# The edge stage of a graph network kernel: gathered rows turned by VectorE and spread by 16 small DMAs instead of being transposed on TensorE

## What is computed

```python
h = maximum(layernorm(x), 0)                       # x: 50000 x 128
gs, gp, gd = rbf @ w_rs, (rbf @ w_rp) * pij, (rbf @ w_rd) * dij    # per edge: 12500 edges, rbf 32, pij 3, dij 5
xx = resmlp0(h)                                    # every node
xs, xp, xd = resmlp1(h)[idx_j], resmlp2(h)[idx_j], resmlp3(h)[idx_j]   # per edge
s = xx + segment_sum(gs * xs, idx_i)
p = segment_sum(gp * xp, idx_i);  d = segment_sum(gd * xd, idx_i)
pa, pb = split(p @ w_pp);  da, db = split(d @ w_pd)
y = s + (pa * pb).sum(-2) + (da * db).sum(-2)
out = x + resmlp4(y)
# resmlp(x) = silu(x + silu(silu(x) @ w1 + b1) @ w2 + b2) @ wout
```

## Time and profile before

| | |
|---|---|
| time, median of 3 runs | 1169.51 us (1167.19 to 1170.66) |
| profiled execution, first to last instruction | 1167.6 us |
| PE, DVE, ACT, POOL busy | 95%, 54%, 65%, 40% of the span |
| node stage | about 0 to 362 us |
| start of the edge stage, PE nearly still | 362 to 379 us |
| edge stage, 25 groups | 379 to 832 us |
| border totals, late blocks and final stage | 832 to 1167.6 us |

### The profile page before, as it was taken

One profiled execution on the slowest core, in us unless ns is written; L12 is line 12 of the kernel. 1 busy time (PEld: TensorE's weight loads), 2 busy tenths in 40 slices (PEclk: granted clock), 3 DMA queues, 4 the chain that ended last, 5 costly groups with the idle time before them and its releaser, 6 DMA issues.

```text
span 1167.6 us, 22917 instructions
## 1 busy us (share of the span) xinstructions
PE 1106.1 (95%) x6787; PEld 751.3 (64%) x6787; DVE 635.5 (54%) x2304; ACT 757.1 (65%) x1423; POOL 463.0 (40%) x426
## 2 busy tenths in 40 slices
PE   3799999899995899999999999999889999999998
PEld 2466766677773466676666666767556666666665
DVE  9999885878762456556565565565512222222222
ACT  2488999789995565655655656555356666666654
POOL 3077773077775346556555565563500000000000
PEclk9999999999998899999999999999999999999999
DMA  8389779477755033333333333334357878888774
GB/s 261 106 264 346 255 254 314 167 232 252 259 180 141 25 66 60 64 59 47 55 49 54 59 50 54 58 44 87 60 176 253 263 254 263 260 249 264 266 241 149
DMA packets 163582, 191.51 MB, mean 164 GB/s; under 512 B 58050, under 2 KB 82538, under 8 KB 163359
## 3 DMA queue, kind: packets, MB, share of 16 engines
q1 hardware_dynamic: 125166, 145.35, 40.6%
q0 software_dynamic: 24208, 19.29, 10.1%
q10 hardware_dynamic: 14112, 25.70, 5.8%
HBM read 94.06 MB, written 96.20 MB: 163 GB/s over the span
## 4 chain that ended last, share of the span: by engine, by line
PE 86%; DVE 9%; DMA 2%; issue 2%; ACT 1%; POOL 0%; SPq 0%; POOLq 0%; ACTq 0%; DVEq 0%
PE bank L1035 8%; PE quad L1023 7%; PE bank L1593 6%; PE bank L858 6%; PE quad L841 6%; PE quad L1027 5%; PE bank L1603 5%; PE bank L1667 4%; PE quad L848 4%; PE bank L1635 4%; PE bank L1668 4%; PE quad L1012 3%; DVE stat L521 2%; PE quad L826 2%; DVE onehot L633 2%; PE quad L1677 2%
## 5 line engine op out<-in xcount | busy, mean ns | idle before, releaser
L1247 POOL DMA_INDIRECT node_sums<-rowout,row_i x98 | 154.9, 1581 | 188.1 <-ACT rowout L1509 165.6
L952 DVE TENSOR_TENSOR rowout<-bank,xin 128x512 f32<-128x512 f32 x98 | 67.8, 692 | 248.7 <-PE bank L1035 248.7
L1035 PEld LDWEIGHTS bank<-wo_sb,s 128*128 128x128 f32 x784 | 102.8, 192 | 47.7 <-issue 47.7
L1280 DVE SCALAR_TENSOR_TENSOR h<-bank,b_sb,hT 128x512 f32<-128x512 f32 (+1 forms) x75 | 55.5, 740 | 138.9 <-PE bank L1603 138.9
L465 POOL DMA_INDIRECT edges_by_src<-pay,rank_i x98 | 99.8, 1019 | 70.9 <-DVE rank_i L662 42.0
L465 POOL DMA_INDIRECT edges_by_low<-pay,rank_i x98 | 98.3, 1003 | 62.1 <-DVE rank_i L662 32.2
L858 PEld LDWEIGHTS bank<-wo_sb,s 128*128 128x128 f32 x720 | 94.7, 192 | 42.9 <-issue 42.9
L751 ACT ACTIVATE xn<-xin,nbias,rnorm 128x128 f32<-128x128 f32 x216 | 103.6, 491 | 14.8 <-DVE nbias L572 14.7
L72 POOL DMA_INDIRECT yin<-node_h,er x98 | 94.7, 967 | 38.1 <-issue 29.2
L1035 PE MATMUL bank<-wo_sb,s 128*128 128x128 f32 x784 | 103.5, 275 | 0.9 <-DVE rowout L952 0.9
L1023 PE MATMUL quad<-s,w_sb 128*128 128x512 f32 x196 | 101.7, 601 | 0.1
(11 more groups left out here) (208 smaller groups left out, 2313.2 us busy)
## 6 DMA issues: line engine op xcount, KB each, us to landing
xin<-in_x_dram SPq DMA_DIRECT2D x196, 256.0 KB, 3.2
node_h<-xn SPq DMA_DIRECT2D x98, 256.0 KB, 2.8
yin<-node_sums SPq DMA_DIRECT2D x98, 256.0 KB, 3.6
out_dram<-rowout ACTq DMA_DIRECT2D x98, 256.0 KB, 3.5
node_sums<-rowout SPq DMA_DIRECT2D x90, 256.0 KB
border_sums_by_tile<-border_sums SPq DMA_DIRECT2D x24, 256.0 KB, 2.0
node_sums<-zeros SPq DMA_DIRECT2D x8, 256.0 KB
edges_by_low<-pay,rank_i POOLq DMA_INDIRECT x98
```

The lines of the kernel that those rows point to most:

```text
L1035: last = nc.tensor.matmul(BANK_O[:, j * P:(j + 1) * P], s3[:, s, j * P:(j + 1) * P], wo_sb[:, m, :], start=True, stop=True)
L1247: nc.gpsimd.indirect_dma_start(out=ysum, out_offset=bass.IndirectOffsetOnAxis(ap=row_i[:, t % 2, j:j + 1], axis=0), in_=urow[:, t % 2, j, ...
```

## The change

Only the edge stage changes in what it does.

- PE no longer transposes gathered rows (except those of group 0), nor the edge features, nor runs the four `pick_src` matmuls.
- DVE turns the gathered rows of group k+1 in 32x32 squares into a new tile `xq` (`squares_T`), at the start of iteration k, ahead of `residual(k,0)`. SP then moves the 4x4 grid of turned squares with 16 SBUF-to-SBUF DMAs (`spread`), each 32 partitions x 128 words, into `hT`. The columns of `hT` now run through the tiles in turn (edge 0 of tiles 0 to 3, edge 1, ...), so what reads a tile's columns as weights (`halves`, `outp(k,2)`), and the two `gate` copies, do so with a step of 4 words.
- `rb` is replaced by `rq`, loaded by one DMA per tile so that DVE's 32x32 transposes make `eR` and `eA` from it directly (`features_T`).
- The sources come as a row: at the start of the stage one DMA copies the 12,544 source words of the table into a DRAM row, word by word, and per group one DMA brings 512 of them to all partitions (`src_in_every_row`).
- The final stage takes over semaphores of the node stage instead of new ones.

```diff
 def load_group(...):
-    eng.dma_start(er[:, s, 0:n, 0:C], rows[:, :, 0:C]).then_inc(indices, 16)
-    eng.dma_start(rb[:, s, 0:n, :], rows[:, :, C:W]).then_inc(done, 16)
+    eng.dma_start(er[:, s, 0:n, :], rows[:, :, 0:C]).then_inc(indices, 16)
+    for t in range(n):
+        tile = by_src[start + t * P:start + (t + 1) * P, :].rearrange("(q r) w -> r q w", r=Q)
+        eng.dma_start(rq[t * Q:(t + 1) * Q, s, :, :], tile).then_inc(done, 16)
...
     def sync(sp):
+        def spread(k):
+            if 1 <= k < G:
+                h, e = k % 2, tiles(k) * Q
+                sp.wait_ge(xq_done, k)
+                if k >= 2:
+                    sp.wait_ge(s1_done, k - 1)
+                    sp.wait_ge(h2_done, 3 * (k - 1))
+                for q in range(P // Q):
+                    for c in range(P // Q):
+                        sp.dma_start(hT[c * Q:(c + 1) * Q, h, q * e:(q + 1) * e],
+                                     xq[q * Q:(q + 1) * Q, h, c * e:(c + 1) * e]).then_inc(hT_in[h], 16)
...
+        def load_src_row(k):
+            if k < G:
+                s, e = k % 2, tiles(k) * P
+                if k >= 2:
+                    sp.wait_ge(same_done, k - 1)
+                sp.dma_start(srow[:, s, 0:e], src_row[0:1, k * BLOCK:k * BLOCK + e].to_broadcast([P, e])).then_inc(srow_in[s], 16)
...
+            sp.dma_start(src_row[0, :].rearrange("(t p) -> t p", p=P), by_src[0:T * P, 0:1].rearrange("(t p) w -> t (p w)", p=P),
+                         allow_slow_non_contiguous=True).then_inc(keys_in, 16)
...
         for k in range(G + 1):
+            spread(k + 1)
             store(k - 2)
             load(k + 2)
+            if k == 0:
+                sp.wait_ge(keys_in, 64)
+                load_src_row(0)
+            load_src_row(k + 1)
...
     def vector(dve):
-        def take_h(k):
+        def squares_T(k):
+            if 1 <= k < G:
+                s, n = k % U, tiles(k)
+                dve.wait_ge(x_in[s], 16 * (TB * (k // U) + n))
+                if k >= 3:
+                    dve.wait_ge(hT_in[k % 2], hT_there(k - 2))
+                nc.vector.transpose(xq[:, k % 2, 0:n * P].rearrange("p (c r t) -> p t c r", t=n, r=Q),
+                                    xg[:, s, 0:n, :].rearrange("p t (c r) -> p t c r", r=Q)).then_inc(xq_done, 1)
...
         for k in range(G + 1):
             t = k - 1
+            squares_T(k + 1)
             if k == 0:
                 key_masks()
             residual(k, 0)
...
-            take_h(k + 1)
+            features_T(k + 1)
...
     def tensor(pe):
-            rows_T(k + 1)
-            edges_T(k + 1)
             outp(k, 2)
...
-                nc.tensor.matmul(BANK_AB[:, 0:2 * F], mT[:, t % 2, 0, cols], wpp_sb[:, :], ...)
+                nc.tensor.matmul(BANK_AB[:, 0:2 * F], by_tile(mT[:, t % 2, 0, 0:n * P], n)[:, j], wpp_sb[:, :], ...)
```

More of the change, by code:

```diff
@@ L190, in rows_there @@
         def rows_there(k):
-            return 48 * (k // U + 1) - (0 if k % U else 16)
+            each = 16 * (TB + 2)
+            short = 16 * (TB - (T - k * TB)) if k == G - 1 and T - k * TB < TB else 0
+            return each * (k // U + 1) - (0 if k % U else 16) - short
         gathered = [sem(f"gathered{i}") for i in range(U)]
@@ L1162, in edge_phase @@
                          "sum_done", "u_in_psum", "u_done", "row_steps", "rows_done"))
+    quads_T, xq_done = sem("edge_features_T"), sem("gathered_quads_T")
+    hT_in = [sem(f"hT_in{i}") for i in range(2)]
+    srow_in = [sem(f"src_row_in{i}") for i in range(2)]
     key_ps, key_done, item_rows, item_ps, item_c, item_steps, item_done = (
@@ L1207, in load_items @@
                 sp.dma_start(items_s[lo:hi, side, :], ssum[lo:hi, side, :]).then_inc(done, 16)
+        with nc.allow_non_contiguous_dma(reason="one word of each row"):
+            sp.dma_start(src_row[0, :].rearrange("(t p) -> t p", p=P), by_src[0:T * P, 0:1].rearrange("(t p) w -> t (p w)", p=P),
+                         allow_slow_non_contiguous=True).then_inc(keys_in, 16)
         with nc.allow_non_contiguous_dma(reason="first and last key of each tile"):
@@ L1476, in gates @@
                 n = tiles(k)
-                for m in range(3):
-                    last = nc.scalar.copy(gate[:, m, 0:n * P].rearrange("p (t e) -> p t e", t=n), quad[:, 0:n, m * P:(m + 1) * P])
-                last.then_inc(gate_done, 1)
+                for m in range(2):
+                    nc.scalar.copy(by_tile(gate[:, m, 0:n * P], n), quad[:, 0:n, m * P:(m + 1) * P])
+                nc.scalar.copy(gate[:, 2, 0:n * P].rearrange("p (t f) -> p t f", t=n), quad[:, 0:n, 2 * P:3 * P]).then_inc(gate_done, 1)
         def halves(t, j):
@@ L1637, in outp @@
                     for j in range(tiles(k)):
-                        last = nc.tensor.matmul(BANK_O[:, j * P:(j + 1) * P], s3[:, m, j * P:(j + 1) * P], wo_sb[:, MLP[m], :], start=True, stop=True)
+                        last = nc.tensor.matmul(BANK_O[:, j * P:(j + 1) * P], by_tile(s3[:, m, 0:tiles(k) * P], tiles(k))[:, j], wo_sb[:, MLP[m], :],
+                                                start=True, stop=True)
                 last.then_inc(o_done, 1)
@@ L1651, in seg @@
                     rows = slice(j * Q, (j + 1) * Q)
-                    nc.tensor.matmul(quad[:, j, 0:2 * P], eA[rows, q, :], ePD[rows, q, :, :].rearrange("p a e -> p (a e)"),
-                                     start=True, stop=True, skip_group_check=True)
-                for j in range(tiles(t)):
-                    rows = slice(j * Q, (j + 1) * Q)
-                    last = nc.tensor.matmul(quad[:, j, 2 * P:3 * P], pick_src[rows, :], eA[rows, q, :], start=False, stop=True, skip_group_check=True)
+                    last = nc.tensor.matmul(quad[:, j, 0:2 * P], eA[rows, q, :], ePD[rows, q, :, :].rearrange("p a e -> p (a e)"),
+                                            start=True, stop=True, skip_group_check=True)
                 last.then_inc(seg_ps, 1)
```

162 lines of the change are left out of this document (84 added, 78 removed).

## The result

| | before | after |
|---|---|---|
| time, median of 4 runs | 1169.1 us (1167.19 to 1170.66) | 1331.74 us (1329.68 to 1334.04) |
| ratio, with its 95% interval | | 1.1395 (1.1376 to 1.1413) |
| first to last instruction, profiled execution | 1167.6 us | 1327.8 us |
| period of a group, residual of group 1 to that of group 23, over 22 | 18.08 us | 23.75 us |

The change made the kernel 162.6 us slower. Slower was forecast, but the time lies 106.7 us above the forecast and 64 above the end of the range.

The account below looks back on a forecast made before the run. PE bounds the edge stage now, at 18.08 us per group; afterwards a ring through SP, POOL and DVE would, its terms summing to 20.7 us. That puts the end 55.5 us later, 1169.5 + 55.5 = 1225 us, range 1174 to 1268.

Parts of the forecast that it names:

- the tail: Rest of groups 23 and 24 behind the residual of group 23: some 1.1 us less on PE.
- The ring: Edge stage: turned rows of k+1, spread, load, gather and turning of k+2 bound the period at 20.7 us; 80%.
- 16 issues of 16 KB DMAs: SP's spread in each round: 16 issues at 0.466 us, priced from DRAM loads of the same shape, 7.46 us.
- 0.47 us each: Sign of being right: the profile would show 16 SP rows of the spread at this length.
- The upper bound, 9.6: Highest price in us for SP's 16 spread issues, from the `rb` issue's pitch of 0.60 us.
- The other terms of the ring: Per round: stores 0.91, `er` and `rq` 2.47, `nxt` 2.2, POOL's start and gathers 6.84, transpose 0.8, SP's start 0.05 us.
- fixed pitch of about 1.28 us: POOL: spacing claimed for each DMA it issues; four gathers take 3.84 us from first to last.
- The row of sources: Stage start: one DMA copying 12,544 source words one by one delays the first groups 0 to 4 us, taken as 0.
- Both bounds (8.5 and 21 us): Lower and upper price of copying the 12,544 source words at the stage start, over at about 385 or 398.
- PE's stepped weights: Rival, 9%: weight loads in `halves` and `outp(k,2)` at twice the time, PE's period 22.0 us, time 1267 us.
- The falling clock: Rival without its own time or chance: PE, resting 3.5 us per group, may lose clock, free while its work fits the period.
- 50 ns of dispatch: Skill's rule for GpSimd's path: 16 DMAs would cost SP 0.8 us, L 14.1, PE setting the pace; not followed.

## Why the prediction was wrong in size

The mechanism was right; two terms of the sum were sized wrong, one in every round and one at the start. Of the 104.8 us by which the forecast of the span fell short (1223 against 1327.8), the 22 rounds carry 71.7 (522.55 against 22 x 20.7 - 0.9 - 3.6 = 450.9 in the forecast, between the same two residuals), the start 30.1 and the tail 2.9.

- **The ring as the new bound: right.** The waits, the idle PE (20.65 of 23.97 us) and the place of each wait are as forecast. Moving the load shortened the round by 4.9 us, four more DMAs lengthened it by what they take to issue.
- **The term "16 issues of 16 KB DMAs", 7.46 us: wrong.** In the round shown they take 10.66, 3.2 of the 3.24 us by which that round exceeds the 20.73 of the sum; the mean of 20 rounds is 10.38. The rows at "0.47 us each" that were to be a sign of being right came at 0.66. The step that failed is the choice of the row: loads of the same shape stood for transfers between partitions of SBUF, and the sentence "that both ends lie in SBUF now is what no row shows" was written without consequence. The upper bound, 9.6, came from a DRAM load too and lies below that mean as well. Over 22 rounds, 2.9 us each are 64 of the 71.7.
- **The other terms of the ring: right.** In order, measured against forecast: stores 1.16 against 0.91, `er` and `rq` 2.45 against 2.47, `nxt` to POOL's start 2.20 against 2.5, three pitches of the gathers 3.86 against 3.84, landing 2.53 against 2.7, transpose and SP's start 1.11 against 0.85. Their errors, up to 0.30 us each, cancel to 0.04, which is luck. The "fixed pitch of about 1.28 us" is that of gathers alone, POOL's adds come every 1.9 us; they lay in the gap all the same.
- **"The row of sources", taken as 0: wrong.** The forecast start was 3.5 us late (383.7 + 20.7 - 0.9 = 403.5 against 400.05), the measured one 33.6. Alone the copy costs 28 us in the profiled execution. Both bounds (8.5 and 21 us) came from DMAs of other kinds: small pieces that were read, and a load of rows. The first was misread besides: 0.09 MB in 1586 packets are 57 bytes each, not words of 4. The step treated the copy as something that runs beside the queue. In fact it kept SP from issuing for 35.80 us, delayed the gathers of group 1 by some 20, and kept PE waiting for the keys until 417.62. The text said that writing DRAM in words "could add more, once", but gave that no place in the range.
- **PE's stepped weights, 9%: real, mis-sized, hidden.** 1.55 us a group, not 4.8; without effect while the ring binds, and what binds next when it is opened.
- **The falling clock without a price: right.** In the round of 23.97 us the mean granted clock was 0.93, so PE ran part of it at 1.2 GHz; PE still had 3.3 us to rest, and the waits that end the round are SP's, POOL's and DVE's. With the load moved ahead, PE didn't rest and the clock was 1.00. That PE was busy 83% of the stage, as forecast (511 of 617 us), is luck: the forecast divides 17.2 by 20.7, and both came out larger.
- **The tail:** 1.8 us more against 1.1 less forecast, no matter.
- **The Trainium skill's 50 ns of dispatch** (DMA: Bandwidth & Descriptors, section Anatomy of one DMA — SWDGE (gpsimd) path) was rightly not used for SP: these rows show 0.465 and 0.64 us per issue.

## What to carry to other kernels

A DMA that is issued by a queue in the middle of a loop is part of every ring that passes through this queue: put loads that somebody waits for ahead of a long row of issues, and let the work that depends on them run one group further ahead, and the row of issues becomes free up to the period. A price must come from a transfer with both ends in the same kind of memory; where there is no such row, the range has to be opened, not only the doubt named. A DMA that writes DRAM word by word is to be charged to its queue and to everything that moves beside it; what one engine makes in 0.22 us per group isn't worth 28 us of copying.

## What the runs showed of the hardware that was not expected

- An issue on SP of a DMA with both ends in SBUF takes 0.62 to 0.66 us (10.20 us for 16 of 32x128 words, 2.47 for 4 of 128x128), in single spreads up to 0.72 (11.53 us for 16); to or from DRAM it takes 0.465 to 0.48. The number of partitions hardly matters, nor whether the words change partition.
- A copy of 12,544 single words from DRAM to DRAM is issued in 0.67 us and then blocks SP's queue for 35.80 us. A copy of 512 words beside four gathers stretches the time from the last gather to its landing from 2.5 to 7.0 us.
- A load of 128x128 fp32 weights takes 0.19 us contiguous and 0.32 to 0.33 with a step of 4 words. A 128x512 transpose in 32x32 squares on DVE takes 0.67 to 0.71 contiguous and 1.08 when it writes with that step.
- A sequencer can be the bound with nothing but issuing: with 28 DMAs a group SP had no pause in a period of 18.12 us.
